# A fifth probability buffer, and attention rows kept in DRAM without gaps

## What is computed

```python
scores = clip(einsum('bhqd,bhkd->bhqk', Q, K), -80, 80)      # 16 heads of 16 + 8 columns
weights = softmax(where(causal, scores, -inf) / sqrt(24))
attn = einsum('bhqk,bhkd->bhqd', weights, V)                 # back to [B, S, 256]
x = x1 + (attn @ W_O) * g                                    # g: the gate of the ffn branch
```

## Time and profile before

| what | value |
|---|---|
| time, median of 3 runs | 2226.02 us (2219.88 to 2229.72) |
| the profiled execution: its time / its span | 2227.83 us / 2226.1 us |
| attention, first to last exponential | 1095.5 to 2137.1 us of the span |
| output stage, to the end of the span | from about 2142.6 us |
| busy share of the span: PE, DVE, ACT, POOL | 90%, 77%, 71%, 29% |
| moved by the DMA engines, mean over the span | 80 GB/s |

### The profile page before, as it was taken

The page is one execution under the profiler, slowest core; times in us unless marked ns, Lnnn a source line. Parts: engine busy times, 40 slices in busy tenths (PEclk is TensorE's granted clock), DMA queues, the critical chain, the costliest instruction groups (busy, mean ns, idle before and its releaser), DMA issues. The chain is left out here.

```text
span 2226.1 us, 54187 instructions
## 1 busy us (share of the span) xinstructions
PE 2009.1 (90%) x23334; PEld 1028.6 (46%) x23334; DVE 1710.6 (77%) x2284; ACT 1579.7 (71%) x1833; POOL 637.8 (29%) x399
## 2 busy tenths in 40 slices
PE   5999999999995788787799999999999999999985
PEld 2655656556553545545433433333343333334343
DVE  7867676676657999999488888888888888888874
ACT  5546445455454555555599999999999999999951
POOL 1645535536445667667100000000000000000025
PEclk9999999999997998999799999999999999999998
DMA  3000101001102555556422222222222222222147
GB/s 99 20 20 20 39 20 30 28 20 39 49 19 90 145 158 166 142 166 169 127 73 78 76 68 70 71 76 73 78 76 67 70 71 76 61 68 64 54 111 263
DMA packets 139149, 178.60 MB, mean 80 GB/s; under 512 B 11552, under 2 KB 109600, under 8 KB 138656
## 3 DMA queue, kind: packets, MB, share of 16 engines
q1 hardware_dynamic: 136880, 172.90, 26.0%
q10 hardware_dynamic: 2032, 2.24, 0.3%
HBM read 91.21 MB, written 83.89 MB: 79 GB/s over the span
## 5 line engine op out<-in xcount | busy, mean ns | idle before, releaser
L1656 ACT ACTIVATE c_probs<-c_ps_b 128x1536 f32<-128x1536 f32 x544 | 858.9, 1579 | 0.0
L1768 PE MATMUL c_ps_o<-c_probs,c_v 128*32 128x256 f32 (+3 forms) x6656 | 581.6, 453 | 3.8 <-DVE c_probs L1688 0.8
L1688 DVE TENSOR_SCALAR c_probs<-c_probs 128x2048 f32<-128x2048 f32 (+2 forms) x415 | 433.9, 1055 | 107.4 <-ACT c_probs L1656 107.4
L1748 PE MATMUL c_ps_a<-c_qk 24*128 24x256 f16 (+2 forms) x2688 | 443.4, 291 | 57.2 <-ACT c_probs L1655 44.2
L1748 PE MATMUL c_ps_b<-c_qk 24*128 24x256 f16 (+2 forms) x8064 | 453.9, 294 | 0.0
L1655 ACT ACTIVATE c_probs<-c_ps_a 128x512 f32<-128x512 f32 x544 | 390.6, 718 | 40.3 <-PE c_ps_o L1768 38.3
L1748 PEld LDWEIGHTS c_ps_a<-c_qk 24*128 24x128 f16 x2688 | 208.7, 92 | 408.4 <-ACT c_probs L1656 207.6
L1917 POOL TENSOR_TENSOR d_prod<-d_prod,d_x 128x1024 f32<-128x1024 f32 x12 | 38.2, 3199 | 1074.4 <-DVE d_prod L1905 1074.4
L1768 PEld LDWEIGHTS c_ps_o<-c_probs,c_v 128*32 128x32 f32 x6656 | 161.5, 108 | 245.3 <-issue 129.4
L258 POOL TENSOR_TENSOR a_hidh<-a_hid,a_hidh 128x512 f16<-128x512 f32 x128 | 169.0, 1338 | 234.9 <-ACT a_hidh L356 230.9
L1748 PEld LDWEIGHTS c_ps_b<-c_qk 24*128 24x128 f16 x8064 | 212.2, 93 | 0.6 <-issue 0.2
(11 more groups left out here) (245 smaller groups left out, 2886.2 us busy)
## 6 DMA issues: line engine op xcount, KB each, us to landing
c_qk<-qk_d SPq DMA_DIRECT2D x256, 96.0 KB
v_d<-b_val SPq DMA_DIRECT2D x16, 1024.0 KB
c_v<-v_d SPq DMA_DIRECT2D x64, 256.0 KB
attn_d<-c_onorm SPq DMA_DIRECT2D x64, 256.0 KB, 2.3
rows<-in_x SPq DMA_DIRECT2D x16, 512.0 KB, 4.8
x_d<-rows_out SPq DMA_DIRECT2D x16, 512.0 KB, 3.2
rows<-x_d SPq DMA_DIRECT2D x16, 512.0 KB, 4.8
qk_d<-b_qc SPq DMA_DIRECT2D x64, 128.0 KB
```

What stands on the lines that cost most here:

```text
L1656: nc.scalar.activation(probs[:, t % NPROB, PARTS[1]], ps_b[:, t % 2], ACT.Exp, scale=unscale).then_inc(exp_b_done, 1)
L1688: nc.vector.tensor_scalar(tile, tile, P_MAX, P_MIN, ALU.min, ALU.max).then_inc(clip_done, 1)
L1748: mm = nc.tensor.matmul(into, k[rows, hk, kt * P:(kt + 1) * P], tokens[rows, hq], start=(i == 0), stop=(i == len(TERMS) - 1), tile_positio ...
L1768: mm = nc.tensor.matmul(ps_o[j * VW:(j + 1) * VW, column:column + w], v[:, kt, j * VW:(j + 1) * VW], probs[:, step % NPROB, j, at:at + w], ...
```

## The change

`NPROB` goes from 4 to 5, so that the exponentials of step t wait for the reader of step t - 5. To make room in SBUF, only four chunks of x1 are read ahead during attention, not six; the other four of the first eight are loaded at the beginning of the output stage. `attn_d` becomes `[DIM, TOKENS]`, 256 rows without gaps. A finished chunk is stored by four transfers, one per head (16 partitions, two runs of 1 KB each), in place of one of 128 partitions. The attention rows of a chunk are read by one transfer of 128 partitions x 2 runs x 2 KB, in place of two transfers of 8 x 16 rows. The counts that the semaphores wait for follow.

```diff
-        "attn": dram("attn_d", [HEADS, VW, TOKENS]),
+        "attn": dram("attn_d", [DIM, TOKENS]),
...
-    return t.rearrange("(k e) r (n t) -> n k e r t", k=KT, t=CH)[:, :, :, 0:D_H]
+    return t.rearrange("(k p) (n t) -> n p k t", p=P, t=CH)
...
-    NPROB = 4
+    NPROB = 5
...
-                    rows = d["attn"][g * GH:(g + 1) * GH, :, b * SEQ:(b + 1) * SEQ].rearrange("e r (n t) -> (e r) n t", t=HALF)
-                    sp.dma_start(rows[:, c::HALVES - 1 - 2 * c][:, 0:2], o_norm[:, e % OUTS, :].rearrange("p (n t) -> p n t", t=HALF)).then_inc(stored[e % OUTS], 16)
+                    for j in range(GH):
+                        head = g * GH + j
+                        rows = d["attn"][head * D_H:(head + 1) * D_H, b * SEQ:(b + 1) * SEQ].rearrange("r (n t) -> r n t", t=HALF)
+                        sp.dma_start(rows[:, c::HALVES - 1 - 2 * c][:, 0:2],
+                                     o_norm[VW * j:VW * j + D_H, e % OUTS, :].rearrange("p (n t) -> p n t", t=HALF)).then_inc(stored[e % OUTS], 16)
...
-                        for k in range(KT):
-                            sp.dma_start(ahead.attn[:, part, k], channel_view(d["attn"])[part, k]).then_inc(ahead.loaded[part], 16)
+                        sp.dma_start(ahead.attn[:, part], channel_view(d["attn"])[part]).then_inc(ahead.loaded[part], 16)
...
-    X_ROWS = 6
+    X_ROWS = 4
...
-        LOADS = 16 * (KT + 1)
+        LOADS = 16 * 2
...
-                    for k in range(KT):
-                        sp.dma_start(attn(s)[:, k], attn_v[s, k]).then_inc(loaded[s], 16)
+                    sp.dma_start(attn(s), attn_v[s]).then_inc(loaded[s], 16)
...
-                        for k in range(KT):
-                            sp.dma_start(attn(n % SLOTS)[:, k], attn_v[n + SLOTS, k]).then_inc(loaded[n % SLOTS], 16)
+                        sp.dma_start(attn(n % SLOTS), attn_v[n + SLOTS]).then_inc(loaded[n % SLOTS], 16)
```

More of the change, by code:

```diff
@@ L1601, in _ @@
                 for s in range(OUTS):
-                    sp.sem_inc(stored[s], 16)
+                    sp.sem_inc(stored[s], 16 * GH)
                 for s in range(2):
@@ L1641, in _ @@
                             for o in range(OUTS):
-                                sp.wait_ge(stored[o], 16 * (GROUPS * CPB // OUTS) + 16)
-                        for k in range(KT):
-                            sp.dma_start(ahead.attn[:, part, k], channel_view(d["attn"])[part, k]).then_inc(ahead.loaded[part], 16)
+                                sp.wait_ge(stored[o], 16 * GH * (GROUPS * CPB // OUTS) + 16 * GH)
+                        sp.dma_start(ahead.attn[:, part], channel_view(d["attn"])[part]).then_inc(ahead.loaded[part], 16)
                 assert rows_loaded >= (NCH + ahead.X_ROWS) * TPC
@@ L1677, in to_channels @@
                     dve.wait_ge(norm_done, e + 1)
-                    dve.wait_ge(stored[e % OUTS], 16 * (e // OUTS) + 16)
+                    dve.wait_ge(stored[e % OUTS], 16 * GH * (e // OUTS) + 16 * GH)
                     nc.vector.transpose(o_norm[:, e % OUTS, :], o_tok[:, e % 2].rearrange("p k r -> p (k r)")).then_inc(ot_done, 1)
@@ L1838, in batch_stored @@
         def batch_stored(batches):
-            return 16 * (batches * GROUPS * CPB // ahead.OUTS) + 16
+            return 16 * GH * (batches * GROUPS * CPB // ahead.OUTS) + 16 * GH
         with nc.Block() as block:
```

## The result

| | before | changed |
|---|---|---|
| median of the runs beside each other | 2225.23 us | 2174.95 us (2173.70 to 2176.74, 4 runs) |
| ratio | | 0.9776, 95% interval 0.9753 to 0.9799 |
| span of the profiled execution | 2226.1 us | 2175.0 us |
| attention, first to last exponential | 1041.6 us | 1005.8 us |
| last exponential to first split of the output stage | 6.1 us | 7.2 us |

The kernel is 2.2% faster; the forecast was 2175 us. The span lost 51.1 us: 35.8 in attention and 16.8 in the output stage, less 1.1 between the two and 0.4 before attention.

A forecast was written before the change was run, and what follows sets the result against it. ACT was taken to set the pace in attention, the DMA engines in the output stage. Attention -36.8, four stores +1.1 and output stage -15.5 sum to -51.2 us, taking 2226.02 to 2175 us; range 2166 to 2194.

The forecast's parts named there:

- Attention: Attention: the fifth buffer removes ACT's 32 waits for values, saving 1.15 of 1.30 us each, -36.8 us.
- PE's long block: Attention, PE: values(9) stands before scores(13) and delays them, so 0.15 us of each 1.30 us is lost again.
- rival 1: Attention: PE doesn't catch up, each of the 32 places keeps 0.43 us; -42.2, 2184 us; chance 0.12.
- rival 3: Attention: the wait only moves, to scores(13); only the output stage gains, -14.4, 2212 us; chance 0.04.
- the clip of step 12: Attention, DVE: it could start at 1511.47 and starts 0.09 later, its reader three steps on; costs nothing.
- Four stores: SP's stores: hidden in attention, but three more issues of 0.37 us behind the last chunk, +1.1 us (0.9 to 1.6).
- Output stage: Output stage: new reads run on all engines, first loads 13.6 us, eight rounds of 4.65 us; -15.5 us.
- rival 2: Output stage: reads of attention rows are limited at DRAM, staying at 141 GB/s alone; -32.6, 2193 us; chance 0.14.
- rival 4: Output stage: reads on 16 engines collide, falling far below 141 GB/s; at 60 GB/s 2250 us; chance 0.02.
- Doubling the old lone rate: Output stage: new reads of attention rows alone taken at twice the old 141 GB/s, 282.
- The forecast's limit of 17 us: Output stage, fastest bound: at 380 GB/s a gain of 19 us, cut by POOL's 16 chunks to about 17.
- The moved x1: Output stage, first loads: four x1 chunks in place of two, 6.2 us in place of 3.1.

The follow-up runs named there:

- experiment 1: Kernel before with five probability buffers and X_ROWS = 4, old layout, stores and reads kept: 2190.22 us, ratio 0.9839.
- experiment 8: Changed kernel with six probability buffers (NPROB = 6) and X_ROWS = 2: 2175.40 us, ratio 0.9782.
- experiment 7: Changed kernel without the put-off second half of a joined step's product, so its output is not the reference's: 2169.27 us, ratio 0.9753.
- experiment 9: Changed kernel with 4 KB of padding behind each row of attn_d, rows 36 KB apart: 2174.04 us, ratio 0.9772.
- experiment 4: Changed kernel with two reads per chunk and 17 rows per head in DRAM, 16 used, so reads are 8 x 16 rows: 2190.53 us, ratio 0.9845.
- experiment 3: Changed kernel with each chunk's attention rows read by two transfers of 128 rows, not one: 2173.83 us, ratio 0.9766.
- experiment 2: Changed kernel with four probability buffers and X_ROWS = 6, new layout, stores and reads kept: 2210.94 us, ratio 0.9930.
- experiment 5: Kernel before, unchanged, profiled once more on the chip of experiment 6, experiment 7 and experiment 8: 2225.42 us.
- experiment 10: Changed kernel with five chunks of x1 read ahead (X_ROWS = 5): 2175.27 us; the changed kernel itself beside it: 2175.53 us; both ratio 0.9774.
- experiment 6: Kernel before with X_ROWS = 4 alone, moving 1 MB of x1 into the output stage: 2227.45 us, ratio 1.0018.

## Why the prediction was right

*Attention (forecast -36.8 us, measured -35.8).* Each step of the working held. ACT's own rhythm stayed at 1.83 us; the wait went whole, which experiments 1 and 8 show; PE's long block then delays the next scores, to 0.16 us against 0.15 forecast, which experiment 7 shows by taking it away; the steps behind it catch up, so rival 1, which would have left 0.43 us in each place, is out, and so is rival 3, a wait that only moves. Per wait 3.137 - 1.834 = 1.303 us were gained and 0.156 lost (means of the unrounded times), 36.7 us for 32. Of the 0.9 us by which attention gained less, 0.7 are a single step: in group 11 (counted from 0) the `values` before the scores of step 14 take 1.83 us and not 1.07, with 0.64 us in their midst in which PE waits for nothing that the profile shows, and ACT's end comes 2.53 us after the one before. The same step is late by as much in experiments 1 and 9, by 0.4 us in 4 and in the changed kernel's second profile, and by at most 0.15 in 3, 8 and with five chunks ahead. I haven't found its cause. For DVE the forecast's working has a slip, without effect: the clip of step 12 could start at 1511.50, not 1511.47. In the changed kernel it starts at 1498.40, 0.03 behind the exponential's end, so nothing is lost there, as forecast.

*Four stores (forecast +1.1 us, measured +1.1).* 6.10 to 7.19 us between the last exponential and the first split, and experiments 1 and 2 put it to the stores. The four issues take 1.70 us and not 4 x 0.37 = 1.48, where the one before took 0.33; some 0.3 us of that come back behind them. In attention they cost nothing, as forecast: 1041.59 us before and 1041.60 in experiment 2.

*Output stage (forecast -15.5 us, measured -16.8).* The mechanism was right: the old reads run at half the share of the DMA engines, the new at the whole. Experiment 4 shows that alone. Rivals 2 and 4, a limit or a collapse at DRAM, are out by the 387 GB/s. But the sum came out by luck in part, as errors in both directions nearly cancelled. Counted from the forecast's starting point (1 us behind the first split, 2109.9), the last of the first loads lands after 13.8 us (13.6 forecast), and the last split starts after 49.4 (50.8 forecast), which leaves 4.45 us for each of the eight rounds (4.65 forecast). Behind these near hits stand:

- The new reads were put at 282 GB/s alone and 330 in the rounds, stores and x1 at 340 to 345. The reads go at 387 and a steady round at 385, so that it takes 4.08 us. Doubling the old lone rate went wrong because the old rate itself was low in that one profile: twice the 190 to 196 of experiments 1, 4 and 5 would have given 380 to 392. The slices with all engines busy were the better row.
- With these rates the forecast's own sum gives 6.2 + 5.4 + 8 x 4.08 = 44.3 us, a gain of 22.0, and 5.1 us of it didn't come. These rows show where they are:

```profile
2109.90:2159.32 49.42, 41.57 (x346) 34.44 (x347) 38.52 (x27) 14.55 (x15) 38.35 (x12) 0.93 1.03 359
2121.45:2145.45 24.00, 22.08 (x196) 18.58 (x194) 22.24 (x15) 6.54 (x7) 23.54 (x8) 1.00 1.01 346
```

- By the first row 17.74 MB are moved before the last split. The forecast counted 16.78: twelve chunks each of rows and x1, and eight stores, but parts of later stores run among the last loads. The other 0.96 MB are about 2.5 us at 385 GB/s (an estimate). The rest, some 2.6 us, is rate: 359 GB/s on the average and 346 in the first 24 us behind the first store, whose pace the additions on POOL set. In experiment 8, where two more loads of x1 are queued by then, the 24 us behind its first store run at 384; those two loads fill the room. No run made the additions faster, so how much of the 2.6 us is POOL's stays open.
- The forecast's limit of 17 us took POOL to hold all sixteen chunks. It holds eight, and the loads hold the rest, so that the measured 16.8 beside it is a coincidence.
- The moved x1 was counted at 3.1 us. With the new reads it costs nothing that shows (experiments 8 and 10): the first store, with which the rounds begin, is issued 12.5 to 12.7 us after the first split whether two, three, four or six chunks of x1 are still to be loaded then (experiments 2, 8 and 10). With the old reads it costs 1 us or a few (experiment 6).

Against the kernel before as profiled in experiment 5 (stage 80.2 us) the stage gains 14.1 us, so part of the 16.8 may be the slower reads of the first profile. The medians don't decide between the two: the rows alone gain 0.70% (0.58 to 0.82), 13 to 18 us, and with the 1.1 us of the four stores added the stage's part is 14 to 19.

*Sum.* -51.2 forecast, -51.1 in the spans, -50.3 in the medians.

## What to carry to other kernels

A wait's listed time is less than what it costs when the engine otherwise overlaps its instructions: measure the distance of the ends with and without it (1.30 us here, where 1.20 was listed), and then walk the next engine through the same step to see what comes late next. When the DMA share of a stretch is about a half while a queue is full, look at how the rows of the transfer are described: a layout whose 128 rows form one dimension moved the same bytes nearly twice as fast, and one unused row per 16 undid it. Price the new pace of a stage with the next engine in view, and count all the bytes that are moved before the point that you forecast: here the rates were 10 to 40% better than forecast, and the stage gained 1.3 us more.

## What the runs showed of the hardware that was not expected

- Loads and stores together ran at 385 GB/s for 16 us, at a share of the DMA engines of 1.08.
- Reads of the same shape from the same program ran at 141 GB/s in one profile and 190 in another, at a share of the DMA engines of 0.54 and 0.56; the cause stays open.
- Exponentials that wait for nothing overlap: the first of a step starts before the second of the step before ends, by 0.32 us (1496.21 against 1496.53) or by 0.11 (1500.24 against 1500.35), and the ends are 1.83 to 1.84 us apart all the same.
